# Loading and rounding the top weights earlier in a DLRM tower kernel

## The reference

```python
e = stack([tbl_f[ids[:, f]] for f in range(27)], axis=1)     # [2048, 27, 128]
x = einsum('bfd,bgd->bfg', e, e)[:, pairs g < f]             # [2048, 351]
h = concatenate([bottom, x, bottom], axis=1)                 # [2048, 607]
h = maximum(h @ W_top1 + b_top1, 0)                          # 512 wide
h = maximum(h @ W_top2 + b_top2, 0)                          # 256 wide
y = h @ W_top3                                               # [2048, 1]
```

## Time and profile before

| | |
|---|---|
| median of 3 runs | 378.96 us |
| profiled execution | 379.7 us, its span 377.9 us |
| PE | 341.6 us busy, 90% |
| POOL | 263.0 us busy, 70% |
| DVE | 248.2 us busy, 66% |
| ACT | 145.9 us busy, 39% |
| chain that ended last | PE 82%, DVE 6%, DMA 4%, ACT 3%, issue 3% |

### The profile page before, as it was taken

How to read it: one execution, slowest core, us unless ns; L and a number is a source line. 1 busy time by engine, 2 the same in 40 slices (tenths; PEclk the granted TensorE clock), 3 DMA queues, 4 the chain that set the end, 5 groups by cost and what they waited for, 6 DMA issues and landing times.

```text
span 377.9 us, 10285 instructions
## 1 busy us (share of the span) xinstructions
PE 341.6 (90%) x4321; PEld 330.9 (88%) x4321; DVE 248.2 (66%) x332; ACT 145.9 (39%) x280; POOL 263.0 (70%) x283
## 2 busy tenths in 40 slices
PE   0667857979899999999999999999999999999996
PEld 0566657979899999999999999999999999998985
DVE  3689994868459918794669546982879456962051
ACT  1467762262531354134431553135313443146202
POOL 6777777777777777777777777777777777773030
PEclk9979998998999999999999999999999999999999
DMA  7987749233724264435333352435343533322230
GB/s 172 232 200 216 193 113 305 68 90 76 241 79 117 68 193 108 107 80 188 111 89 84 94 201 72 105 74 191 104 104 81 187 112 89 82 63 73 51 29 1
DMA packets 46905, 45.76 MB, mean 121 GB/s; under 512 B 32944, under 2 KB 35782, under 8 KB 46860
## 3 DMA queue, kind: packets, MB, share of 16 engines
q1 hardware_dynamic: 35950, 27.04, 26.9%
q0 software_dynamic: 8896, 17.89, 17.0%
q10 hardware_dynamic: 2014, 0.18, 0.4%
HBM read 39.52 MB, written 5.55 MB: 119 GB/s over the span
## 4 chain that ended last, share of the span: by engine, by line
PE 82%; DVE 6%; DMA 4%; ACT 3%; issue 3%; SPq 1%
PE work L441 41%; PE gram L468 14%; PE work L453 6%; PE work L494 4%; PE work L495 4%; PE work L496 4%; DMA raw_lo<-in_tbl 4%; DVE onehot L601 3%; PE work L511 2%; PE work L513 2%; PE work L512 2%; PE work L522 2%; DVE tab_lo L586 2%; SPq L331 1%; DVE w_lo L611 1%
## 5 line engine op out<-in xcount | busy, mean ns | idle before, releaser
L411 POOL DMA_INDIRECT emb<-in_tbl,ids_all x272 | 259.1, 953 | 84.0 <-issue 80.2
L601 DVE TENSOR_TENSOR onehot<-ids_bc,row_idf 125x1024 fp32r<-125x1024 int32 (+2 forms) x232 | 199.0, 919 | 38.2 <-PE work L441 32.6
L441 PE MATMUL work<-onehot,tab_hi 125*128 125x256 f32 x672 | 172.7, 296 | 24.9 <-ACT tab_hi L707 13.0
L441 PE MATMUL work<-onehot,tab_lo 125*128 125x256 f32 x672 | 168.9, 290 | 2.5 <-issue 2.5
L441 PEld LDWEIGHTS work<-onehot,tab_hi 125*128 125x128 f32 x672 | 133.5, 199 | 33.5 <-issue 18.5
L441 PEld LDWEIGHTS work<-onehot,tab_lo 125*128 125x128 f32 x672 | 133.9, 199 | 0.0
L749 ACT COPY embT<-work 128x512 f32<-128x512 f32 (+1 forms) x36 | 26.8, 797 | 103.3 <-PE work L441 103.3
L468 PE MATMUL gram<-embT 128*54 128x52 f32 x1920 | 51.5, 214 | 2.4 <-ACT embT L571 2.2
L468 PEld LDWEIGHTS gram<-embT 128*54 128x54 f32 x1920 | 49.5, 130 | 4.7 <-issue 1.4
L756 ACT COPY inter<-gram 118x416 f32<-118x416 f32 x64 | 32.4, 507 | 16.7 <-PE gram L468 15.8
L494 PE MATMUL work<-x_hi,w_hi 128*128 128x256 f32 (+1 forms) x128 | 36.9, 288 | 1.8 <-DVE embT L571 0.9
(11 more groups left out here) (55 smaller groups left out, 220.5 us busy)
## 6 DMA issues: line engine op xcount, KB each, us to landing
ids_bc<-in_sel_ids SPq DMA_DIRECT2D x14, 512.0 KB, 4.4
grams<-inter SPq DMA_DIRECT2D x64, 84.5 KB
emb<-in_tbl,ids_all POOLq DMA_INDIRECT x272
ids_bc<-in_sel_ids SPq DMA_DIRECT2D x11, 256.0 KB, 8.6
misc<-in_tbl SPq DMA_DIRECT2D x3, 448.0 KB
inter<-in_tbl SPq DMA_DIRECT2D x3, 448.0 KB
misc<-in_bottom SPq DMA_DIRECT2D x8, 128.0 KB
raw_w<-in_W_top SPq DMA_DIRECT2D x4, 256.0 KB, 7.4
```

The source lines that it names most:

```text
L411: pool.indirect_dma_start(out=emb[:, t % TILE_SLOTS, f, :], out_offset=None, in_=gather_tables[f], in_offset=bass.IndirectOffsetOnAxis(ap= ...
L441: mm = nc.tensor.matmul(out, part[0:k, CHUNK_AT[f] + c, :], onehot[0:k, at % RING, i * HALF:(i + 1) * HALF], start=(c == 0 and i % 2 == 0 ...
L601: nc.vector.tensor_tensor(onehot[0:k, at % RING, 0:width], ids_bc[0:k, four[0]:four[-1] + 1, :].rearrange("p i n -> p (i n)"), row_idf[0:k ...
```

## The change

SP issues the weights of a chunk behind each of the last three tables (chunk CH behind table 7 of the order, chunk 2 with the bias behind table 8, chunk 1 behind table 9), and chunk 0 and W_top2 behind the first ids of half 1. DVE sums the two bottom blocks ahead of the sixth one-hot of half 1, apart from the splits, which stay where they were. ACT rounds all weights behind the extraction of gram 0 and ahead of half 1's first select_out.

```diff
@@ sync
+                if n >= NSEL - 3:
+                    load_w1(X_ORDER[n - (NSEL - 3)])
                 if n == 3:
                     sp.dma_start(ids_all[:, 2:, :], ids_v[:, 2:ID_SLOTS, :]).then_inc(ids_loaded[1], 16)
...
             for j, (four, _, _) in enumerate(FOURS):
                 sp.wait_ge(onehot_ready, ...)
                 load_ids(1, j)
+                if j == 0:
+                    load_w1(X_ORDER[CH])
+                    sp.dma_start(raw_w2[:, 1, :, :], w_top2.rearrange("(c p) n -> p c n", p=P)).then_inc(w2_loaded, 16)
             sp.wait_ge(table_hi, NSEL)
             sp.wait_ge(table_lo, len(PIECES))
             sp.dma_start(bot[:, :, :], bottom_v[0]).then_inc(bot_loaded, 16)
-            load_weights()
@@ vector
+            def sum_w1_bottom():
+                dve.wait_ge(w1_loaded[CH], 32)
+                nc.vector.tensor_tensor(raw_w1[:, 1, CH, :], raw_w1[:, 1, CH, :], raw_w1[:, 0, CH, :], ALU.add).then_inc(w1_bot_summed, 1)
...
             for n in range(len(ONEHOTS[1])):
+                if n == RING:
+                    sum_w1_bottom()
                 if n == 8 + RING:
                     for c in X_ORDER:
                         split_w1(c)
@@ scalar
             extract_all(0)
+            for c in X_ORDER:
+                round_w1(c)
+            round_w2()
             select_out(1, 0)
             extract_all(1)
             rows_all(2)
-            for c in X_ORDER:
-                round_w1(c)
-            round_w2()
```

More of the change, by code:

```diff
@@ L318, in _, with load_w1 @@
         def _(sp):
+            def load_w1(c):
+                if c == CH:
+                    sp.dma_start(raw_w1[:, 1, CH, :], w_top1[0:D, :]).then_inc(w1_loaded[CH], 16)
+                    sp.dma_start(raw_w1[:, 0, CH, :], w_top1[D + PAIRS:, :]).then_inc(w1_loaded[CH], 16)
+                else:
+                    sp.dma_start(raw_w1[0:PAIR_ROWS[c], 1, c, :], w_top1[D + c * P:D + c * P + PAIR_ROWS[c], :]).then_inc(w1_loaded[c], 16)
+                if c == CH - 1:
+                    sp.dma_start(raw_w1[ONES:ONES + 1, 1, c, :], b_top1.rearrange("(o n) -> o n", o=1)).then_inc(w1_loaded[c], 16)
             sp.dma_start(ids_all[:, 0:2, :], ids_v[:, 0:2, :]).then_inc(ids_loaded[0], 16)
@@ L339, in load_ids @@
                 sp.dma_start(ids_bc[:, some, :], sel_ids[h][:, some, :].to_broadcast([P, len(four), HALF])).then_inc(ids_bc_loaded[j], 16)
-            def load_weights():
-                for c in X_ORDER:
[L344 to L351, removed]
             def store(t):
@@ L603, in one_hot @@
                                         row_idf[0:k, ROW_AT[chunks] + c:ROW_AT[chunks] + c + 1].to_broadcast([k, width]), ALU.is_equal).then_inc(onehot_ready, 1)
+            def sum_w1_bottom():
+                dve.wait_ge(w1_loaded[CH], 32)
+                nc.vector.tensor_tensor(raw_w1[:, 1, CH, :], raw_w1[:, 1, CH, :], raw_w1[:, 0, CH, :], ALU.add).then_inc(w1_bot_summed, 1)
             def split_w1(c):
                 k = X_ROWS[c]
-                if c == CH:
-                    dve.wait_ge(w1_loaded[c], 32)
-                    nc.vector.tensor_tensor(raw_w1[:, 1, c, :], raw_w1[:, 1, c, :], raw_w1[:, 0, c, :], ALU.add).then_inc(w1_bot_summed, 1)
                 dve.wait_ge(w1_hi_ready, X_ORDER.index(c) + 1)
```

## The result

| | before | after |
|---|---|---|
| median | 379.05 us (22 runs) | 377.9 us (22 runs, 377.07 to 379.69) |
| profiled execution, its span | 379.7, 377.9 us | 377.67, 375.8 us |
| ratio after to before | | 0.9967, 95% interval [0.9954, 0.9979] |

The change takes 1.25 us off (0.0033 x 379; interval 0.8 to 1.7). Inside the kernel PE gained six to seven times as much. Lines of the changed kernel stand one lower on PE and POOL (L442 selects, L454 transposes, L469 products, L412 gathers).

A forecast was written before the change was run, and what follows sets the result against it. PE holds most of the chain of waits, but POOL's gathers are as much at their limit; of PE's 4.1 us only 1.0 survives tile 15. So 379.7 - 1.0 = 378.7, and with the profile 0.7 above the median, 378.0 us; range 376.3 to 380.0.

The forecast's parts named there:

- POOL is the floor, and PE runs into it: POOL's 272 gathers run without a hole at 1.25 us each; PE's gain ends in waits at tiles 13 and 15.
- PE's gain, 4.1 us: By the end of select(1, 2): 2.12 us of stall, 1.7 us of half clock and some 0.3 us of small waits.
- The stall at 82 us: PE waits 2.12 us for rounding, remainders and the next one-hot; the change was to remove it and the half clock behind.
- The stall at 60.7 us: PE's unexplained 2.54 us stall under saturated DMA; moving loads might gain 0 to 2.5 + 1.7 us, taken as 0.
- The distance, 1.0 us: How far PE is behind POOL's last gather at tile 15, all it can gain; 2.2 us kept for the range.
- POOL's price for the remainders, between -0.9 and +0.9 us: Gathers stretched beside DVE's weight work may change POOL's time by that much either way; taken as 0.
- ACT and DVE: Roundings after 60.5 us end by 63.8, hidden ahead of half 1's select_out; DVE's 0.63 us sum is hidden before a one-hot.
- The expected smaller spread: Runs before spread over 2.7 us; the changed kernel should spread less, as POOL's chain hardly differs between executions.
- Rival (a): At tile 15's products, PE's new wait halves the clock and costs 1.7 us, giving 379.7 us; chance 0.30.
- Rival (b): PE's whole gain comes through because gathers land or issue earlier: 374.9 us, or 371; chance 0.08.
- Rival (c): Tables 8 and 9 or W_top2 load too late, PE losing over 3.1 us; 380.9 at 6 us lateness; chance 0.05.
- Rival (d): No difference, as the median run before was already bound by POOL: 379.0 us; chance 0.12.

The follow-up runs named there:

- a_skip14: The changed kernel with the last gather of tiles 2 to 15 left out, so its output is wrong; 372.47 us, ratio 0.9824.
- b_skip14: The kernel before with the last gather of tiles 2 to 15 left out, so its output is wrong; 379.49 us, ratio 1.0015.
- psum_last1: The changed kernel with gathers grouped 4, 4, 4, 4, 1 and the weights' remainders taken by way of PSUM; 377.46 us, ratio 0.9943.
- fill_best: The changed kernel regrouped 4, 4, 4, 4, 1, remainders by way of PSUM, two fourths of half 6's mlp1 moved into PE's waits at tile 15; 378.98 us, ratio 0.9988.
- load_only: The changed kernel with ACT's and DVE's part undone, so only SP's early weight loads remain; 378.36 us, ratio 0.9981.
- order_only: The changed kernel with SP's part undone, so only ACT's early rounding and DVE's early sum remain; 378.88 us, ratio 0.9983.
- b_iota36: The kernel before with 36 small iotas on POOL ahead of tile 2's gathers, lengthening its chain; 385.94 us, ratio 1.0162.
- a_iota: The changed kernel with 12 small iotas on POOL ahead of tile 2's gathers, lengthening its chain; 380.34 us.
- b_iota: The kernel before with 12 small iotas on POOL ahead of tile 2's gathers, lengthening its chain; 381.33 us, ratio 1.0081.
- a_iota36: The changed kernel with 36 small iotas on POOL ahead of tile 2's gathers, lengthening its chain; 384.87 us.

## Why the prediction was right

The median came out at 377.9 us and was forecast at 378.0. The mechanism was right. That the number agrees to 0.1 us is partly luck, as the third step shows. Step by step:

**POOL is the floor, and PE runs into it: right.** The forecast said that PE's gain would end in waits for the last group of the odd tiles, and that the gathers would stay without a hole. Both are in the profile, and a_skip14 with b_skip14 show it as a cause.

**PE's gain, 4.1 us: half of it.** The stall at 82 us went as it should, and the early rounding is worth 3.9 us. The forecast had the sum right and a part of it wrong: the half clock was to cost 1.7 of the 4.1 us, and it costs 0.5; the rest is PE going at the pace of the one-hots behind the stall. The stall at 60.7 us was bounded by 0 and 4.2 us and taken at 0. It went too, and was worth the whole 4.2. The forecast said that this would not matter, and it did not: PE only ran into POOL at tile 3 already, instead of tile 11. Nor does the half clock always follow. b_skip14's profiled execution has both stalls (2.21 and 2.13 us), no lower clock behind them, and took 377.03 us, the fastest of its kernel.

**The distance, 1.0 us: too small by half in the profile, near the medians by luck.** In the profile it was 2.06 us, close to the upper bound kept for the range. POOL's last gather ends 0.5 us earlier (344.08 instead of 344.57). The group was ready 2.05 us after the last gather's end, where I had put 2.5 to 2.6 from the last single packet of its queue; with that landing PE's distance was 1.5 us and not 1.0. The forecast then carried over that the profiled execution before lay 0.7 us above the median. A kernel that POOL bounds doesn't keep that distance: after, the profiled execution (377.67) lies 0.2 us below the median of 377.9. The two errors nearly cancel, and the runs give 1.25 us. The Trainium skill ("DMA: Bandwidth & Descriptors", section on the anatomy of one DMA on the gpsimd path) gives 2.0 us and the bytes at 436 GB/s; the estimate from it, 2.15 us from the start of the gather, is too short here as well: the chain after has 2.96 us from the start at 343.13 to the landing.

**POOL's price for the remainders, between -0.9 and +0.9 us: right, and the reason is now known.** The changed kernel had three gathers of 1.39 to 1.43 us beside the sum and the remainders. psum_last1 and fill_best show it to be the second operand in SBUF: with PSUM in its place no gather beside a remainder is stretched, and none of over 1.0 us stands anywhere but beside an instruction with both operands in SBUF.

**ACT and DVE: right.** ACT rounds at 59.82 and is done at 62.9, 4.3 us ahead of its select_out, which comes 4.7 us earlier than before. The sum stands at 57.94, in front of an idle DVE. Table 9 is first read at 45.94 us right behind ACT's other work, as before, so the loads delayed no selection. The expected smaller spread came too: 377.07 to 379.69 us after, 377.74 to 381.77 before.

**Rival (a), 0.30: it is real, and it isn't the usual execution.** It did not happen in the profiled execution of the changed kernel (clock 1.00 from 348.3 to 351.8). It did in those of load_only, order_only and b_iota36, where the products took 4.99, 4.66 and 5.00 us instead of 3.41. It did not in those of a_iota, b_iota and a_iota36, which had waited 1.23, 1.40 and 1.14 us for the gather and 1.05 for the copy. Five of the changed kernel's 22 runs lie at 378.75 us or more, the other 17 at 377.07 to 378.25. That those five had the lower clock there is argued from the distance and from the profiled executions of the variants, and not shown. Their mean granted clocks (0.984, and 0.993 four times) aren't below those of the others (0.984 to 0.997), so on record nothing singles them out; a stretched gather (2.55 us in load_only) moves the end as well.

**Rival (b)** needed gathers to come earlier than they can; a_skip14 is what it would have looked like. **Rival (c)** did not occur. **Rival (d)**, no difference, is out by the interval, 0.8 to 1.7 us, and by b_skip14: the median of the kernel before did not hang on POOL.

## What to carry to other kernels

Ask of every engine how long its chain is, not how busy it is: POOL was busy 70%, and nearly all of its gaps were the 0.30 us between two gathers. Then measure how far the engine on the critical path is behind that chain at the last place where they meet; a faster critical path is worth that distance and no more. And before idle time on PE is filled with other work, look what that work covers where it stands now. When a forecast meets the number, redo it with each measured term: here a distance too small by half and a carried-over 0.7 us made up for each other.

## What the runs showed of the hardware

- An indirect gather of 128 rows of 512 bytes costs POOL 0.945 us and 0.30 us to the next, whatever the DMA queues carry: in the kernel before the period was 1.25 us at a DMA share of 1.06 (60.5 to 64 us) and of 0.25 (82.8 to 84.5 us). Its data were there 2.75 (psum_last1) to 3.04 us (b_iota) after its start.
- DVE additions and subtractions of float32 with both operands in SBUF stretched gathers beside them, up to 2.55 us (load_only); all 68 gathers of over 1.0 us in the 14 profiles, first ones aside, stand beside such an instruction. The same subtraction with one operand in PSUM stretched none (psum_last1, fill_best).
- Two idle stretches of PE with 0.66 us of work between them were followed by 1.2 GHz in some executions (1.21 and 1.05 us in load_only) and by 2.4 GHz in others (1.40 and 1.05 us in b_iota). Of the ten single ones of 1.9 to 3.2 us near 60 and 82 us, three were followed by 1.2 GHz (2.12 and 2.54 us in the kernel before, 2.73 in order_only) and seven by 2.4 GHz, among them the longest (3.17 us, b_iota). The length doesn't tell which.
- The half clock behind the stall at 60.7 us cost PE 1.6 us (15.40 us from products to products with a stall of 2.54, 14.54 us in b_iota with one of 3.17 and the full clock, 11.22 without either). Behind the one at 82 us, where DVE set the pace, it cost 0.5 us.
- While weights filled the DMA engines (share 1.02 to 1.08), PE stood 2.2 to 3.2 us without any semaphore to wait for, in all five profiled kernels that loaded them at that time.
